# One program for three phases, with step 0 of attention begun in the last block of the first feed-forward phase

## The chip, the core and the metric

The kernel runs on one core of a Trainium2 chip. A core has five engines that run their own instruction queues in order and meet only at semaphores: TensorE (PE: multiplications and transposes; PEld is its weight load), VectorE (DVE), ScalarE (ACT), GpSimd (POOL), and SyncE (SP), which issues the transfers. The metric is the device time of one execution in microseconds (us).

## What is computed

A "macaron" layer over 4 sequences of 512 tokens, 256 wide, in float32: half a feed-forward step, attention, half a feed-forward step, each on the layer-normed x.

```python
x = x + 0.5 * ffn(layernorm(x))
x = x + attn(layernorm(x))
x = x + 0.5 * ffn(layernorm(x))
# ffn: 8 experts, silu(x @ W_e + b_e), the two best by the router's logits, weighted by a softmax,
#      then @ proj_w + proj_b, residual y = x + out, and RMS norm of y times norm_w
# attn: 16 heads of 128 in 4 groups that share a key and a value head, rotary embedding of q and k,
#       keys scaled by a weight per head, causal softmax, values, then @ wo.T
```

## The kernel before

Every multiplication is done in three parts: both operands are split into a rounded lead and a rest (names end in `hi`/`h` and `lo`/`l`), and lead x lead, lead x rest and rest x lead are summed in PSUM. ScalarE writes a lead (a copy that rounds), and VectorE or GpSimd subtracts it from the source to get the rest.

**Feed-forward** (`ffn_phase`, called twice: names f1_ and f2_). A body runs for each of the 4 blocks (sequences). A block has two halves g, and four pairs p of experts; a unit is one pair for 128 tokens. TensorE fills a ring of four PSUM banks with units, ScalarE takes the silu in place, VectorE adds the weighted halves into `acc` (`weighted`, L464), and TensorE may refill a bank when its unit is summed. Half a block later `acc` is transposed (`sum_T`, L794), split, and projected (`project`, L807 to L809); VectorE adds the residual, ScalarE squares, GpSimd raises to -0.5 (`inverse_rms`), VectorE scales (`scale_rows`) and GpSimd adds the rows into x (`add_rows`). Beside it run the layer norm of later blocks (`norm_stats`, `rstd`, `norm_rows`, `transpose_z`, `z_lead`, `z_rest`), the router, and, in the first phase, the split of attention's weights: the `group_lead` pieces on ScalarE and `group_rest` pieces on GpSimd, four pieces for each of four groups. Three groups go to a buffer in DRAM, `attn_split`, and group 0, the last, stays in `wa` and `gb` but for its output weights, which are stored from `gc` and loaded again by attention. The last block also normalises the two blocks 0 and 1 of attention, the second (j = BATCH + 1) by VectorE's z rows at L384 in the second half of the block.

The first phase ends with `step_project(0)` to `(5)`: key, four queries and value of step 0, each six matmuls of 128x512 into a bank of its own, which `step_out` on ScalarE copies to `ga` (raw) or `vT`. SyncE copies the halves of every raw part to `gc`, swapped, for the rotary embedding.

**Attention** (`attention_phase`, names at_). 16 steps, one for each group and sequence, of 4 heads. For each step the five raw parts (key and four queries) are rotated on GpSimd (raw x cos, swapped x sin, sum: L1063, L1065, L1069), their leads are written by ScalarE (L1291), their rests by GpSimd (L1054). A head is `scores`, `mask_min` on VectorE (L1152), `exps` on ScalarE (L1306), `normalise` on VectorE (L1161), `transpose_p`, leads and rests of the transposed probabilities, `weigh`, and `output`. Heads overlap: scores of head n + 2 stand beside the weighting of head n. Steps 1 to 14 run in hardware loops. Step 0 has its own start: rotations 0 and 2 and the rests 0, 1 and 2 on VectorE (`early_cos`, `early_sum`, `early_rest`: L1232 to L1243), rotations 1, 3 and 4 and the other rests on GpSimd.

**The order** is written out by hand, engine by engine. The three phases are three blocks of the language, with buffers and PSUM banks of their own beside a shared set; between two blocks all five engines meet at a barrier. Each block's first instructions set its constants and load ScalarE's table.

## Time and profile before

| | us |
|---|---|
| median of 3 runs | 856.11 |
| the runs | 856.01 to 856.42 |
| the profiled execution | 854.68 |
| its span | 852.8 |
| TensorE busy in the span | 802.1 (94%) |
| VectorE busy | 673.2 (79%) |
| ScalarE busy | 504.6 (59%) |
| GpSimd busy | 509.4 (60%) |

The span is what the profiler sees from first to last instruction; the time of the execution has 1.9 us around it. The first phase lasts to about 157 us, attention to about 721 us, the second feed-forward phase to the end. The page gives sums; the timeline gives each instruction's start and length and, in brackets, how long its engine was idle before it and what ended that. "PEq" or "DVEq" as releaser is the sequencer of the engine, here the barrier.

### The profile page before, as it was taken

How to read it: one execution, taken by the hardware profiler on the slowest of the kernel's cores; microseconds unless marked ns; L12 is line 12 of the kernel's file. 1: busy time of each engine (PE TensorE's matmuls, PEld its weight loads, DVE VectorE, ACT ScalarE, POOL GpSimd, SP SyncE). 2: the span in 40 equal slices, each digit the busy share in tenths (PEclk: the TensorE clock that was granted, in tenths of full speed). 3: DMA queues.
4: the chain of work that ended last, by engine and by line, in shares of the span. 5: the costliest groups of instructions: out<-in, count | busy, mean ns of one | idle time of the engine just before them, and what ended most of it. 6: DMA issues, size and time to landing. Idle time of an engine off the chain costs nothing. (4 is left out here: it accounts for less than half of the span.)

```text
span 852.8 us, 16061 instructions
## 1 busy us (share of the span) xinstructions
PE 802.1 (94%) x4712; PEld 702.2 (82%) x4712; DVE 673.2 (79%) x1929; ACT 504.6 (59%) x1241; POOL 509.4 (60%) x401
## 2 busy tenths in 40 slices
PE   7899997667999999999999999999999998899995
PEld 4688876556999999899999999999999997688884
DVE  5998996799786876966977868769678797988874
ACT  3455553355576765765766767658658674445442
POOL 4536632557777787777787877877877740312211
PEclk9899998879999999999999999999999999999997
DMA  9145411500212311312312213122221100000001
GB/s 300 51 149 185 139 48 58 141 13 13 51 38 61 99 25 37 98 30 68 98 25 49 74 37 86 37 74 49 74 49 44 30 13 1 1 1 25 25 1 50
DMA packets 29558, 52.19 MB, mean 61 GB/s; under 512 B 3922, under 2 KB 9682, under 8 KB 29522
## 3 DMA queue, kind: packets, MB, share of 16 engines
...
## 5 line engine op out<-in xcount | busy, mean ns | idle before, releaser
L1166 DVE TENSOR_TENSOR at_ptl<-at_pt,at_pth 128x512 fp32r<-128x512 f32 (+1 forms) x192 | 108.9, 594 | 47.1 <-ACT at_pth L1312 47.0
L1312 ACT ACTIVATE at_pth<-at_pt 128x512 fp32r<-128x512 f32 (+1 forms) x192 | 94.2, 525 | 84.8 <-PE at_pt L1470 84.8
L1306 ACT ACTIVATE at_pr<-at_pr,at_low 128x512 f32<-128x512 f32 (+3 forms) x256 | 140.6, 557 | 2.3 <-DVE at_low L1152 2.2
L1054 POOL TENSOR_TENSOR at_ql<-at_rot,at_qh 128x512 fp32r<-128x512 f32 x62 | 79.8, 1288 | 96.7 <-ACT at_qh L1291 96.7
L610 ACT ACTIVATE f_ex<-f_ex 128x512 f32<-128x512 f32 x128 | 74.5, 583 | 90.9 <-PE f_ex L782 90.3
L464 DVE SCALAR_TENSOR_TENSOR f_acc<-f_ex,f_full,f_acc 128x256 f32<-128x256 f32 x224 | 95.8, 477 | 26.2 <-ACT f_ex L610 25.4
L1161 DVE TENSOR_SCALAR at_pr<-at_pr,at_inv 128x128 f32<-128x128 f32 (+3 forms) x256 | 110.9, 494 | 2.3
L1069 POOL TENSOR_TENSOR at_rot<-at_rot,gc 128x512 f32<-128x512 f32 x78 | 101.5, 1302 | 8.1 <-POOLq L1086 2.1
L1063 POOL TENSOR_TENSOR at_rot<-ga,cos 128x512 f32<-128x512 f32 x78 | 102.0, 1308 | 4.1 <-POOL at_ql L1054 2.4
L1065 POOL TENSOR_TENSOR gc<-gc,sin 128x512 f32<-128x512 f32 x78 | 102.4, 1313 | 0.0
L1470 PE MATMUL at_pt<-ident,at_pr 128*128 128x128 f32 x640 | 94.2, 278 | 7.6 <-DVE at_pr L1161 6.7
L1152 DVE CUSTOM_DVE_ANT_0 at_pr<-at_sc,at_mask 128x512 f32<-128x512 f32 (+2 forms) x192 | 100.5, 547 | 0.0
L780 PE MATMUL f_ex<-f_e_hi,zh 128*128 128x512 f32 x224 | 93.5, 418 | 6.5 <-DVE f_acc L464 6.4
L1291 ACT ACTIVATE at_qh<-at_rot 128x512 fp32r<-128x512 f32 x64 | 40.5, 633 | 91.8 <-POOL at_rot L1069 89.7
L781 PE MATMUL f_ex<-f_e_hi,zl 128*128 128x512 f32 x224 | 90.9, 406 | 0.0
L782 PE MATMUL f_ex<-f_e_lo,zh 128*128 128x512 f32 x224 | 90.9, 406 | 0.0
L1484 PE MATMUL at_o<-at_pth,at_vh 128*128 128x512 f32 (+3 forms) x256 | 83.0, 324 | 0.1
L1486 PE MATMUL at_o<-at_pth,at_vl 128*128 128x512 f32 (+3 forms) x256 | 82.6, 323 | 0.0
L1485 PE MATMUL at_o<-at_ptl,at_vh 128*128 128x512 f32 (+3 forms) x256 | 82.4, 322 | 0.0
L1470 PEld LDWEIGHTS at_pt<-ident,at_pr 128*128 128x128 f32 x640 | 71.3, 143 | 10.4 <-DVE at_pr L1161 7.6
L1459 PE MATMUL at_sc<-at_keys,at_ql 128*128 (+4 forms) x256 | 78.7, 318 | 0.0
L1457 PE MATMUL at_sc<-at_keys,at_qh 128*128 (+3 forms) x192 | 71.9, 375 | 5.4 <-DVE at_ql L1243 5.4
...
## 6 DMA issues: line engine op xcount, KB each, us to landing
gc<-ga SPq DMA_DIRECT2D x160, 128.0 KB, 2.3
at_wo<-attn_split SPq DMA_DIRECT2D x8, 512.0 KB, 4.3
...
gb<-attn_split SPq DMA_DIRECT2D x6, 512.0 KB, 4.2
...
x<-in_x SPq DMA_DIRECT2D x4, 512.0 KB, 8.7
...
```

What stands on the lines that cost most here:

```text
L464: dve.scalar_tensor_tensor(out=acc[:, tile, :], in0=h, scalar=full_w[:, tile, e:e + 1], in1=acc[:, tile, :], op0=ALU.mult, op1=ALU.add).th ...
L780: pe.matmul(o, zh[:, c, tok], hi[:, :, w], start=(c == 0), stop=False)
L781: pe.matmul(o, zl[:, c, tok], hi[:, :, w], start=False, stop=False)
L1063: pool.tensor_tensor(rot[r % 2][:], raw[r], cosT[:], ALU.mult)
L1065: pool.tensor_tensor(swap[r], swap[r], sinT[:], ALU.mult).then_inc(sin_done, 1)
L1069: pool.tensor_tensor(rot[r % 2][:], rot[r % 2][:], swap[r], ALU.add).then_inc(sum_done, 1)
L1152: dve.tensor_tensor_reduce(out=out, in0=sc[bank][:, col:col + w], in1=masked, scale=1.0, scalar=3e38, op0=ALU.add, op1=ALU.min, accum_out= ...
L1161: dve.tensor_scalar(a, a, inv[h % 2][:, i:i + 1], None, ALU.mult).then_inc(nm_done, 1)
L1166: dve.tensor_tensor(ptl[h % 2][:, cols], pt[(NF * h + k) % 2][:, 0:FLEN[k]], pth[h % 2][:, cols].bitcast(F32), ALU.subtract).then_inc(lo_d ...
L1306: act.activation(pr[h % 2][:, cols], pr[h % 2][:, cols], ACT.Exp, bias=low[h % 2][:, i:i + 1], scale=-1.0, accum_out=tot[h % 2][:, i:i + 1 ...
L1312: act.activation(pth[h % 2][:, cols], pt[(NF * h + k) % 2][:, 0:FLEN[k]], ACT.Copy).then_inc(hi_done, 1)
L1470: r = pe.transpose(pt[(NF * h + k) % 2][:, col + (i - kt) * P:col + (i - kt + 1) * P], pr[h % 2][:, OFF[i] + kt * P:OFF[i] + (kt + 1) * P] ...
```

## The change

1. There is one block. The phases are now functions (`feed_forward`, `attention`) that return a program for each engine, and each engine runs the three in a row. Where two interleave, a program is a generator that stops at `yield`. Both barriers go, and with them the constants' second and third setting.
2. The eight PSUM banks have one set of names (`pj`, `sc`, `pt`, `o`) and each phase maps its own onto them. All but the last projection of step 0 go through the bank `pj1`; each waits until ScalarE has copied the one before. Buffers in SBUF are laid out anew (`ROOMS` leaves space), so that step 0 can write while the first phase still reads.
3. Projections 0, 1 and 2 of step 0 stand inside the last block's second half. ScalarE's leads of the rotated key and first query stand there too, among the silus, and VectorE's rests of them. The last projections, scores of heads 0 and 1, and the tail of the last block are interleaved.
4. GpSimd does all five rotations of step 0, VectorE the rests 0, 1 and 2, GpSimd the rests 3 and 4.
5. The split of group 0 begins with the output weights, written straight to `wo`: two stores and two loads of 512 KB go. Slots of the last group move: 25, 26, 27, 28.
6. The statistics and rows of the last extra normalisation come earlier in VectorE's queue.
7. At the end of attention, the second phase's table load, the lead and rest of expert pair 1 and its first router multiplication are put into the last attention step.

```diff
+ROOMS = (256, 2800, 384)
...
 
-        SLOTS = ((3, 4, 5, 6), (9, 10, 12, 13), (17, 18, 20, 21), (25, 26, 28, 29))
+        SLOTS = ((3, 4, 5, 6), (9, 10, 12, 13), (17, 18, 20, 21), (25, 26, 27, 28))
 
         def piece_at(i, g, p):
...
@@ -320,10 +319,13 @@
                     scale_queries(i)
                 if first:
                     group_rest(i, 0)
+                if first and i == LAST:
+                    rstd(BATCH + 1)
+                if first:
                     group_rest(i, 1)
                 if i > 0:
                     inverse_rms(i - 1, 1)
-                if i + 2 < NORMS:
+                if i + 2 < NORMS and i < LAST:
                     rstd(i + 2)
                 if i > 0:
                     add_rows(i - 1, 1)
...
@@ -512,10 +516,14 @@
                     add_residual(i - 1, 1)
                 if i + 1 < NORMS:
                     z_rest(i + 1)
+                if first and i == LAST:
+                    norm_stats(BATCH + 1)
                 weighted(i, 0, 3)
                 if i > 0:
                     mean_square(i - 1, 1)
-                if i + 2 < NORMS:
+                if first and i == LAST:
+                    norm_rows(BATCH + 1)
+                elif i + 2 < NORMS:
                     norm_stats(i + 2)
                 if first and i == 0:
                     dve.wait_ge(p_hi_done, 1)
@@ -524,8 +532,6 @@
                 if i > 0:
                     scale_rows(i - 1, 1)
                 sum_rest(i, 0)
-                if i == LAST and NORMS > BATCH:
-                    norm_rows(BATCH + 1)
                 weighted(i, 1, 1)
                 if i < LAST:
                     choose(i + 1)
@@ -535,11 +541,13 @@
                 if i < LAST:
                     weigh_chosen(i + 1)
                 add_residual(i, 0)
+                if first and i == LAST:
+                    early_rest(dve, 0)
                 weighted(i, 1, 3)
                 mean_square(i, 0)
-
-            if not first:
-                dve.sem_inc(e_lo_done, 1)
+                if first and i == LAST:
+                    early_rest(dve, 1)
+
             if first:
                 dve.memset(r_hl[:].bitcast(F32), 0.0).then_inc(setup, 1)
                 dve.memset(r_h0[:].bitcast(F32), 0.0).then_inc(setup, 1)
...
@@ -643,11 +665,10 @@
 
                 act.wait_ge(step_done, k + 1)
                 if k < NR:
-                    if k == 0:
-                        act.wait_ge(a_lo_done, PIECES * KV)
-                    act.activation(raw[k], step_ps[k][:], ACT.Copy).then_inc(raw_done, 1)
+                    act.wait_ge(a_lo_done, PIECES * KV - (1 if k < 2 else 0))
+                    act.activation(raw[k], t_ps[1][:], ACT.Copy).then_inc(raw_done, 1)
                 else:
-                    act.activation(vT[:], step_ps[k][:], ACT.Copy).then_inc(vt_done, 1)
+                    act.activation(vT[:], pj[0][:], ACT.Copy).then_inc(vt_done, 1)
 
             def body(i):
                 silu(i, 0, 0, 0)
@@ -681,23 +702,33 @@
                 group_lead(i, 1, 0)
                 silu(i, 1, 0, 1)
                 sum_lead(i, 0)
+                if first and i == LAST:
+                    step_out(0)
                 silu(i, 1, 1, 0)
                 group_lead(i, 1, 1)
                 silu(i, 1, 1, 1)
-                if i == LAST and NORMS > BATCH:
+                if first and i == LAST:
                     z_lead(BATCH + 1)
+                    step_out(1)
                 silu(i, 1, 2, 0)
+                if first and i == LAST:
+                    rotated_lead(act, 0, 0)
                 if i < LAST:
                     half_tanh(i + 1)
                 group_lead(i, 1, 2)
                 silu(i, 1, 2, 1)
+                if first and i == LAST:
+                    step_out(2)
                 silu(i, 1, 3, 0)
                 squares(i, 0)
+                if first and i == LAST:
+                    rotated_lead(act, 0, 1)
                 silu(i, 1, 3, 1)
 
             if not first:
                 act.sem_inc(e_hi_done, 1)
-            act.wait_ge(half_set, 2)
+            if first:
...
@@ -812,19 +843,27 @@
             def step_project(k):
 
                 if k == 0:
-                    pe.wait_ge(zlo_done, C * NORMS)
-                    pe.wait_ge(a_lo_done, PIECES * KV)
-                elif k < NR:
-                    pe.wait_ge(acc_done, sums_of(UNITS * BATCH - RING + k - 1))
+                    pe.wait_ge(zlo_done, C * (BATCH + 1))
+                    pe.wait_ge(a_lo_done, PIECES * KV - 2)
+                elif k == NR:
+                    pe.wait_ge(raw_done, NR + 1)
                 else:
-                    pe.wait_ge(raw_done, 1)
+                    pe.wait_ge(raw_done, k)
+                    pe.wait_ge(a_lo_done, PIECES * KV - (2 if k < 2 else 0))
                 (hi, lo), w = ((wa[:, 0], wa[:, 1]), k) if k < 2 else (wb, k - 2)
                 w = slice(w * HD, (w + 1) * HD)
+                bank = (pj[0] if k == NR else t_ps[1])[:]
                 for c in range(C):
-                    pe.matmul(step_ps[k][:], hi[:, c, w], zh[:, c, 0:SEQ], start=(c == 0), stop=False)
-                    pe.matmul(step_ps[k][:], hi[:, c, w], zl[:, c, 0:SEQ], start=False, stop=False)
-                    r = pe.matmul(step_ps[k][:], lo[:, c, w], zh[:, c, 0:SEQ], start=False, stop=(c == C - 1))
+                    pe.matmul(bank, hi[:, c, w], zh[:, c, 0:SEQ], start=(c == 0), stop=False)
+                    pe.matmul(bank, hi[:, c, w], zl[:, c, 0:SEQ], start=False, stop=False)
+                    r = pe.matmul(bank, lo[:, c, w], zh[:, c, 0:SEQ], start=False, stop=(c == C - 1))
                 r.then_inc(step_done, 1)
+
+            def ring_free():
+                pe.wait_ge(acc_done, sums_of(UNITS * BATCH - RING))
+
+            def rows_scaled(g):
+                pe.wait_ge(xn_done, BT * LAST + HT * (g + 1))
 
             def body(i):
                 if i > 0:
@@ -843,11 +882,16 @@
                 sum_T(i, 0)
                 if i < LAST:
                     logits_back(i + 1)
+                elif first:
+                    step_project(0)
                 experts(i, 1, 1)
-                if i == LAST and NORMS > BATCH:
+                if first and i == LAST:
                     transpose_z(BATCH + 1)
+                    step_project(1)
                 experts(i, 1, 2)
                 project(i, 0)
+                if first and i == LAST:
+                    step_project(2)
                 experts(i, 1, 3)
 
             if first:
...
@@ -1097,14 +1131,19 @@
             rest(STEPS - 1, NR - 1)
             rstd(2)
 
-        @block.vector
-        def _(dve):
+        def offsets(dve):
             dve.sem_inc(wa_in, WA0)
             dve.sem_inc(wb_in, WB0)
+            dve.sem_inc(wo_in, WO0)
             dve.sem_inc(lo_done, LO0)
             dve.sem_inc(ol_done, OL0)
 
+        def vector(dve, tail, last_pairs):
+            sum_rest, scale_rows, add_residual, mean_square, add_last_rows, rows_final = tail
+
             def norm_stats(k, b, _):
+                if k < 2:
+                    rows_final(b)
                 if k == 2:
                     dve.wait_ge(xu_done, 2 * (STEPS - BATCH + b + 1))
                 for t in range(BT):
...
+            last_block = BATCH - 1
+            sum_rest(last_block, 1)
             dve.wait_ge(mask_in, 16)
             mask_min(0, 0)
+            early_rest(dve, 2)
+            scale_rows(last_block, 0)
             norm_stats(*NORMS[0])
+            add_residual(last_block, 1)
             normalise(0, 0)
+            mean_square(last_block, 1)
             mask_min(1, 1)
+            scale_rows(last_block, 1)
+            add_last_rows()
+            value_rest(0)
             prob_rest(0, 0, 0)
             prob_rest(0, 0, 1)
+            normalise(1, 1)
+            prob_rest(0, 0, 2)
             norm_stats(*NORMS[1])
-            normalise(1, 1)
-            value_rest(0)
-            prob_rest(0, 0, 2)
             step(0, True, False)
             with dve.Fori(1, STEPS - 1) as s:
                 step(s, False, False)
             step(STEPS - 1, False, True)
             add_output(STEPS - 1, part=1)
 
-        @block.scalar
-        def _(act):
...
-            act.activation(warm[:], mhalf[:], ACT.Exp).then_inc(half_set, 1)
-            rotated_lead(0, 0)
-            rotated_lead(0, 1)
+                        last_pairs()
+
+            act.activation(warm[:, 2], mhalf[:], ACT.Exp)
+            step_out(3)
+            sum_lead(BATCH - 1, 1)
+            rotated_lead(act, 0, 2)
+            step_out(4)
+            exps(0, 0)
+            squares(BATCH - 1, 1)
             raw_out(1, 0)
+            rotated_lead(act, 0, 3)
+            step_out(NR)
             raw_out(1, 1)
-            rotated_lead(0, 2)
-            rotated_lead(0, 3)
-            exps(0, 0)
+            exps(1, 1)
             value_lead(0)
-            raw_out(1, 2)
             prob_lead(0, 0, 0)
             prob_lead(0, 0, 1)
-            rotated_lead(0, 4)
-            exps(1, 1)
+            raw_out(1, 2)
+            rotated_lead(act, 0, 4)
             prob_lead(0, 0, 2)
             step(0, True, 2)
             with act.Fori(1, STEPS - 2) as s:
@@ -1381,8 +1414,9 @@
             step(STEPS - 2, False, 1)
```

The second half of block 3 on ScalarE, from the lead of its first sums (`f1_ch`), before; `f1_ex` and later `pj`, `sc` are the ring's banks, `f1_t` and `pt`, `o` the others:

```order
L614 ACTIVATE f1_ch<-f1_t0 128x512 [waits f1_ct_done]
L610 ACTIVATE f1_ex2<-f1_ex2 128x512 [waits f1_ex_done]
L640 ACTIVATE gc<-ga 128x1024 [waits f1_a_in3,f1_a_in2]
L610 ACTIVATE f1_ex3<-f1_ex3 128x512 [waits f1_ex_done]
L586 ACTIVATE zh<-f1_t0 128x512 [waits f1_tz_done]
L586 ACTIVATE zh<-f1_t1 128x512 [waits f1_tz_done]
L610 ACTIVATE f1_ex0<-f1_ex0 128x512 [waits f1_ex_done]
L610 ACTIVATE f1_ex1<-f1_ex1 128x512 [waits f1_ex_done]
L610 ACTIVATE f1_ex2<-f1_ex2 128x512 [waits f1_ex_done]
L620 ACTIVATE f1_sq,f1_ss<-f1_wide0 128x256 [waits f1_yadd_done]
L620 ACTIVATE f1_sq,f1_ss<-f1_wide0 128x256
L610 ACTIVATE f1_ex3<-f1_ex3 128x512 [waits f1_ex_done]
```

And after:

```order
L634 ACTIVATE f1_ch<-pt0 128x512 [waits f1_ct_done]
L669 ACTIVATE ga<-pj1 128x512 [waits f1_a_lo_done,f1_step_done]
L630 ACTIVATE sc1<-sc1 128x512 [waits f1_ex_done]
L630 ACTIVATE sc2<-sc2 128x512 [waits f1_ex_done]
L606 ACTIVATE zh<-pt0 128x512 [waits f1_tz_done]
L606 ACTIVATE zh<-o 128x512 [waits f1_tz_done]
L669 ACTIVATE ga<-pj1 128x512 [waits f1_a_lo_done,f1_step_done]
L630 ACTIVATE pj0<-pj0 128x512 [waits f1_ex_done]
L1298 ACTIVATE at_keys<-at_rot0 128x512 [waits at_sum_done]
L630 ACTIVATE sc0<-sc0 128x512 [waits f1_ex_done]
L669 ACTIVATE ga<-pj1 128x512 [waits f1_a_lo_done,f1_step_done]
L630 ACTIVATE sc1<-sc1 128x512 [waits f1_ex_done]
```

Two copies of raw projections to `ga` and the lead of the rotated key stand ahead of the last silus; before, all six copies came behind them.

GpSimd at the same place, before, from the power for the norm of block 5 (`f1_rs`):

```order
L267 TENSOR_TENSOR f1_rs<-f1_ve,f1_mhalf 128x4 [waits f1_ln_var]
L308 TENSOR_TENSOR x<-x,f1_y 128x512 [waits f1_xn_done]
L298 TENSOR_TENSOR gb<-ga,gb 128x512 [waits f1_a_hi_done]
L298 TENSOR_TENSOR gc<-ga,gc 128x1024 [waits f1_a_hi_done]
L303 TENSOR_TENSOR f1_rr<-f1_ms,f1_mhalf 128x2 [waits f1_rms]
L308 TENSOR_TENSOR x<-x,f1_y 128x512 [waits f1_xn_done]
L303 TENSOR_TENSOR f1_rr<-f1_ms,f1_mhalf 128x2 [waits f1_rms]
L77 UNCONDITIONAL_BRANCH
L1048 UNCONDITIONAL_BRANCH [waits barrier_Pool_Activation_PE_DVE_SP_gather]
L1081 MEMSET at_mhalf 128x4
L1063 TENSOR_TENSOR at_rot1<-ga,cos 128x512 [waits at_half_set,raw_done]
```

And after, from the rest of the piece `wa`:

```order
L297 TENSOR_TENSOR wa<-ga,wa 128x512 [waits f1_a_hi_done]
L302 TENSOR_TENSOR rr<-ms,mhalf 128x2 [waits f1_rms]
L307 TENSOR_TENSOR x<-x,f1_y 128x512 [waits f1_xn_done]
L297 TENSOR_TENSOR gb<-ga,gb 128x512 [waits f1_a_hi_done] x2
L1100 TENSOR_TENSOR at_rot0<-ga,cos 128x512 [waits raw_done]
L1102 TENSOR_TENSOR gc<-gc,sin 128x512 [waits swap_in0]
L1104 TENSOR_TENSOR at_rot0<-at_rot0,gc 128x512 [waits at_sin_done]
L1100 TENSOR_TENSOR at_rot1<-ga,cos 128x512 [waits raw_done]
L1102 TENSOR_TENSOR gc<-gc,sin 128x512 [waits swap_in1]
L1104 TENSOR_TENSOR at_rot1<-at_rot1,gc 128x512 [waits at_sin_done]
L302 TENSOR_TENSOR rr<-ms,mhalf 128x2 [waits f1_rms]
```

The rotations (L1100 to L1104) follow the last pieces directly, and the power for the last block's first half (`rr`) stands behind two of them.

TensorE in the last attention step, after: the end of the output multiplication of three heads, the router's four, and the weighting of head 3 (`at_pth1`); before, the router's rows stood behind the barrier:

```order
L1549 MATMUL pj1<-at_wo1,at_oh 128x256
L1550 MATMUL pj1<-at_wo0,at_ol 128x256
L783 MATMUL sc2<-zh,r_hl 128x512 [waits at_zlo_done]
L784 MATMUL sc2<-zl,r_h0 128x512
L783 MATMUL sc2<-zh,r_hl 128x512
L784 MATMUL sc2<-zl,r_h0 128x512
L1518 MATMUL o<-at_pth1,at_vh 128x512 [waits at_lo_done,at_ol_done]
L1519 MATMUL o<-at_ptl1,at_vh 128x512
```

The router waits for the rests of the normalised rows (`at_zlo_done`) in the middle of the attention step.

## Rows read from the trace of the kernel before

**Rows 1.** Page, parts 1 and 2: busy time; busy tenths in 40 slices of 21.3 us.
```profile
PE 802.1 (94%) x4712; PEld 702.2 (82%) x4712; DVE 673.2 (79%) x1929; ACT 504.6 (59%) x1241; POOL 509.4 (60%) x401
...
PE   7899997667999999999999999999999998899995
...
POOL 4536632557777787777787877877877740312211
```

**Rows 2.** Waits of PE, 120 to 240 us: us in total, times, longest.
```profile
PE f_t L735 <- DVE z L384: 5.7, 1, 5.7
PE at_pt L1470 <- DVE at_pr L1161: 5.6, 2, 4.1
PE at_sc L1457 <- DVE at_ql L1243: 5.4, 1, 5.4
PE at_pj L1396 <- DVE z L1124: 4.0, 1, 4.0
PE at_pj L1405 <- DVEq L1102: 1.9, 1, 1.9
```

**Rows 3.** Windows: us, busy us of each engine, PEclk, DMA share, GB/s.
```profile
173.00:190.00 17.00, 10.56 (x41) 8.59 (x40) 16.59 (x48) 8.97 (x25) 10.69 (x9) 0.71 0.07 15
...
400.00:420.00 20.00, 20.00 (x130) 18.32 (x129) 15.38 (x47) 13.50 (x36) 16.58 (x14) 1.00 0.19 49
```

**Rows 4.** Timeline of PE at the first seam: start us, us, engine, line, instruction, [idle before].
```profile
126.05 0.60 PE L794 MATMUL f_t<-ident,f_acc 128*128 128x128 f32 x4
...
144.98 0.39 PE L824 MATMUL f_t<-zh,wa 128*128 128x512 f32 x1
...
146.36 0.40 PE L824 MATMUL f_ex<-zh,wa 128*128 128x512 f32 x1
...
165.55 0.79 PE L1457 MATMUL at_sc<-at_keys,at_qh 128*128 128x512 f32 x1 [5.38 <-DVE at_ql L1243]
...
180.17 0.78 PE L1457 MATMUL at_sc<-at_keys,at_qh 128*128 128x512 f32 x1
```

**Rows 5.** Timeline of DVE, 130 to 190 us, the same columns.
```profile
128.83 0.87 DVE L492 SCALAR_TENSOR_TENSOR f_y<-f_wide,f_rr,rows 128x256 f32<-128x256 f32 x2
...
130.21 4.91 DVE L384 TENSOR_SCALAR z<-x,f_mv,f_rs 128x256 f32<-128x256 f32 x4
...
189.05 1.37 DVE L1124 TENSOR_SCALAR z<-x,at_mv,at_rs 128x256 f32<-128x256 f32 x4
```

**Rows 6.** Page, part 5: groups of ACT, all through the program.
```profile
L1306 ACT ACTIVATE at_pr<-at_pr,at_low 128x512 f32<-128x512 f32 (+3 forms) x256 | 140.6, 557 | 2.3 <-DVE at_low L1152 2.2
```

**Rows 7.** Timeline of POOL, 127 to 160 us.
```profile
127.42 1.01 POOL L267 TENSOR_TENSOR f_rs<-f_ve,f_mhalf 128x4 f32<-128x4 f32 x1 [1.22 <-DVE f_ve L372]
...
157.34 1.29 POOL L1063 TENSOR_TENSOR at_rot<-ga,cos 128x512 f32<-128x512 f32 x1 [0.18 <-POOL at_mhalf L1081]
158.58 1.74 POOL L1065 TENSOR_TENSOR gc<-gc,sin 128x512 f32<-128x512 f32 x1
```

**Rows 8.** Issues of DMAs, 120 to 200 us: count, KB each, median us to landing.
```profile
gc<-ga SPq DMA_DIRECT2D x16, 128.0 KB, 2.3
...
at_wo<-attn_split SPq DMA_DIRECT2D x2, 512.0 KB, 4.9
```

**Rows 9.** Timelines of PE, DVE and ACT at the second seam.
```profile
721.48 0.47 PE L756 MATMUL f_t<-zh,r_hl 128*128 128x512 f32 x1 [1.05 <-PEq L900]
...
732.64 0.47 PE L780 MATMUL f_ex<-f_e_hi,zh 128*128 128x512 f32 x1 [3.31 <-DVE f_acc L464]
...
728.22 2.35 DVE L425 TENSOR_SCALAR f_w<-f_th 128x4 f32<-128x4 f32 x1
...
717.06 0.60 ACT L1316 ACTIVATE at_oh<-at_o 128x512 fp32r<-128x512 f32 x1 [3.39 <-PE at_o L1486]
721.51 1.28 ACT L701 ACT_TABLE_LOAD   x1 [3.85 <-PEq L900]
...
722.91 1.04 ACT L605 ACTIVATE f_e_hi<-e_raw 128x1024 fp32r<-128x1024 f32 x1
```

406 lines of the change are left out of this document (225 added, 181 removed).

## The prediction

> **What bounds the kernel now.** I read the page first. TensorE is busy 94% of the span, and its strip in 40 slices is at 9 nearly everywhere; the holes lie at slices 7 to 10 (128 to 213 us) and again near slice 35 [rows 1]. So only work that stands in TensorE's way at those holes can shorten the span. The windows confirm the contrast: at 400 to 420 us TensorE is busy all 20.00 us at a granted clock of 1.00, at 173 to 190 us it is busy 10.56 of 17 us at 0.71 [rows 3]. Then the list of TensorE's waits from 120 to 240 us says what the holes are: 5.7 us for the normalised rows of the block that step 0 will read, 1.9 us for the barrier between the first feed-forward phase and attention, 5.4 us for the first rests of rotated keys and queries, 5.6 us for normalised probabilities, 4.0 us for the z rows of a later block, together 22.6 us [rows 2]. Last, the timelines show why. From 135 to 157 us GpSimd is almost empty (its strip falls to 5 and 3 tenths there) [rows 1], yet the rotations of step 0, which are GpSimd's kind of work, begin at 157.34, behind the barrier [rows 7]; TensorE reaches the first scores of step 0 at 165.55 and the third scores (head 2) at 180.17 [rows 4]. The second seam is small: 1.05 us before TensorE's router multiplication and 3.31 us later for the first weighted sums [rows 9].
>
> I call the time of the start of the third scores the milestone. Behind it step 0 runs as before, so what the milestone gains, the span gains.
>
> **The change at the first seam, in order of time on the clock of the trace before.** Work is moved, hardly any is removed: six projections of 1.38 us each (144.98 to 146.36) [rows 4], two barriers, two stores of 512 KB and their two loads back. TensorE pays the same multiplications, so the gain is waiting alone, and I follow the chain.
>
> Start: sum transposes at 126.05 [rows 4]. VectorE now does the statistics of the extra normalisation (about 2.0 us) before the weighted sums that this transpose waits for, and GpSimd holds the piece of wa behind the power for that normalisation (1.01 us) [rows 7]. I estimate 0.6 and 0.4 us of new TensorE waiting; the first projection ends near 128.9.
>
> The normalised rows themselves took 4.91 us at 130.21, when GpSimd was running three multiplications and subtractions beside them, and 1.37 us at 189.05 when it was not [rows 5]. In the new order they stand earlier, when GpSimd has one short piece to do; I take 1.8 us, so the 5.7 us wait goes. What is late next is the last pieces of the weight split: GpSimd adds the scaled rows first. These were scaled by 129.7 (128.83 and 0.87) [rows 5]; with 1.3 us more of VectorE work ahead, 131.0. Add 1.3 us for the addition and 1.3 us for the piece: 133.6. ScalarE's copy of projection 0 waits for that piece, since it overwrites its source, and all of ScalarE's queue, two silus first, waits behind it. The copy is out at 134.2. TensorE, with one bank for all projections, waits 1.5 us for it. Then TensorE is busy to 145.3.
>
> Rotation 0: the half swap lands some 3.1 us after the copy (issue 0.6, 2.3 to landing [rows 8], 0.2 between); then sine product and addition, 1.3 us each as the cosine product took 1.29 [rows 7]: 139.9. ScalarE waits for it ahead of the silu of unit 13, so the weighted sums slip. By the order of ScalarE's queue (lead 0, silu, copy 2, silu, squares, lead 1, silu) its last silu ends at 145.2, the last weighted sum at 146.5, the rest of query 0 at 147.3. The first scores start there, against 165.55.
>
> Then the gain shrinks, since VectorE now does only the rests and GpSimd all five rotations. Rotation 2 is queued behind the power for the last rows: start 147.35, three operations of 1.3, end 151.3. ScalarE waits for it ahead of the exponentials of head 0: four at 0.557 mean [rows 6], 2.3 us, 154.8. The squares of the last rows wait on VectorE's addition (statistics of another block stand before it) to 156.3; squares, power, and only then rotation 3: 158.4 to 162.3. ScalarE waits for rotation 3 ahead of the value copy and the exponentials of head 1; these end at 166.4, value lead and rest, the first probability rest at 168.4. The milestone is at **168.6** against 180.17: a gain of 11.6 us. Two of the operations in the chain may run at the 1.74 us of 158.58 rather than 1.29 [rows 7], 0.9 us: I take 11.
>
> Cover: with three loads fewer on the queue the swaps meet less traffic; the mask load, moved ahead, has some 10 us until it is used. If all TensorE waits of the seam went, the gain would be 17.1 us of idle (5.7, 1.9, 5.4 and the longest of 4.1 before probabilities [rows 2]) and, I estimate from the granted clock of 0.71 in 17 us [rows 3], about 4 us of slow matmuls: 21 us. If only the barrier went, it would be 1.9 us. I take 11, nearest to the row-by-row chain.
>
> After the milestone the wait of 4.0 us for z rows stays: it is VectorE beside GpSimd's rotations, and those stand there as before.
>
> **The change at the second seam.** The router's four matmuls go ahead of the last weighting, so the barrier wait of 1.05 us goes [rows 9] and nothing on TensorE is added. VectorE then can choose experts right after the logits, with the second pair's split behind it already, an operation of the length of ScalarE's 1.04 us for the same elements [rows 9]: weights 1.0 us earlier, the wait of 3.31 us falls to about 2.3. The 2.35 us for a 4-element product at 728.22 [rows 9] stays, since GpSimd's residual starts at the same event. ScalarE's table load (1.28 us) and the split of 1.04 us now stand ahead of the last lead of attention; ScalarE was idle 3.39 us there [rows 9], they take 2.5, so nothing is late. Gain 2.0 us, bounds 1 and 4.4.
>
> On that cover the trace shows the load at 1.28 us with the next instruction right behind it. The Trainium skill, page "ScalarE: Activation LUTs", section "What ACT_TABLE_LOAD costs", adds a drain and gives 2.66 us for a switch; by it ScalarE would be 0.5 us late there and the second seam would give 1.5 us. The measured row decides for me.
>
> **Sum.** 11 and 2 us: 13 us. The profiled execution took 854.68 us, span 852.8 and 1.9 around it; its new span would be 839.8. The median of the runs is 856.11, 1.4 above the profiled one; from the median I predict 843.1 us.
>
> **Rivals.**
> First, the forecast: gain of 9 to 17 us, 839 to 847 us, chance 0.60.
> Second, more: ScalarE's waits ahead of silus and exponentials hurt less than I laid out, because rotations end before ScalarE comes to them, and the z wait of 4.0 us [rows 2] moves to where GpSimd is idle. 13, 4 and 2 us of slower clock: 19 us, 837 us; chance 0.13. For it: those waits are in my arithmetic, not in the trace. Against: GpSimd's three queued operations per rotation are firm.
> Third, less: the swap of rotation 0 takes 4.9 us as the large loads do [rows 8], 2.6 more, and GpSimd's chained operations run at 1.74, twelve times 0.45, of which half is on the path: 5.3 us back, 848.4 us; chance 0.15, as far as 853.
> Fourth, slower: VectorE and GpSimd block each other. Four z rows took 4.91 instead of 1.37 us beside GpSimd, 0.9 us each [rows 5]. From 126 to 168 us the new order puts some 20 VectorE operations of these kinds (z rows, rests, normalised probabilities, the row addition) near 15 operations of GpSimd which used to run before or behind. If 15 of the 20 are hit and all on the path, 13.5 us go and the gain is spent; with all 20 it is 18 us and 861 us. Chance 0.07. For it: the sizes are measured. Against: most of these stand where the chain waits for GpSimd anyway.
> The Trainium skill, page "SBUF — State Buffer", section "SBUF: two separate sides", says this as a rule that speaks against the change: VectorE's fast modes, and its operations with two SBUF inputs against a GpSimd reader, take one port pair by turns for whole instructions. The 4.91 us agree with it; it gives no price of its own.
> Fifth, within 0.2%: chain and seams cancel, 0.05.
>
> **How the numbers follow.** About 0.2%, 1.7 us, is what a measurement of this kernel can tell from no change. Faster 0.88, same 0.05, slower 0.07. The range leaves out the slower cases and the ends of the second and third: 835.5 to 851.
>
> **What would show it.** Right: no barrier gap at 155 us; first scores near 147 us, third scores between 167 and 172; router matmuls inside the last attention step; the wait for weighted sums in the second phase 2 to 3 us; the middle of attention unchanged pass for pass. Wrong: third scores after 176 us, or ScalarE idle under 1 us ahead of the leads of rotations 0, 2 and 3, or any change of the attention loop's pass time.

## The result and the profile after

The changed kernel took **842.86 us** (median of 4 runs, 841.95 to 843.60) against 856.06 us (4 runs, 854.50 to 856.42): a ratio of **0.985, 95% interval 0.983 to 0.987**. Forecast were 843.1 us and the range 835.5 to 851. The profiled execution took 843.1 us, its span is 841.1 (before 854.68 and 852.8), so the traces differ by 11.7 us.

Page of the changed kernel, parts 1 and 2, the lines of [rows 1]:

```profile
PE 796.0 (95%) x4712; PEld 699.4 (83%) x4712; DVE 659.6 (78%) x1923; ACT 503.2 (60%) x1241; POOL 513.7 (61%) x403
...
PE   7899998777999999999999999999999999899995
...
POOL 4545736775778778777777787877777750312211
```

TensorE has the same 4,712 multiplications. Its hole in the eighth to tenth slice reads 777 where it read 667, and the seventh slice reads 8 where it read 7. Waits of TensorE from 120 to 240 us in the changed kernel, the answer to [rows 2] (us in total, times, longest; the rows from 1.2 us up):

```profile
PE pj L1430 <- DVE z L1163: 6.8, 2, 3.9
PE pj L857 <- ACT ga L1321: 2.5, 1, 2.5
PE pt L1504 <- DVE at_ptl L1205: 1.9, 2, 1.5
PE pj L1474 <- ACT vT L671: 1.9, 1, 1.9
PE pt L1504 <- DVE at_pr L1200: 1.6, 1, 1.6
PE pj L857 <- ACT ga L669: 1.6, 1, 1.6
PE pt L823 <- DVE f_acc L468: 1.3, 2, 1.0
PE pj L1439 <- DVE zl L1174: 1.2, 2, 1.0
```

The barrier, the 5.7 us for the normalised rows of the first phase and the 5.4 us for the first rests are gone. Other waits stand in their place: ScalarE's copies of the projections (`ga`, `vT`), and z rows of later blocks, 6.8 us where there were 4.0. TensorE's timeline in the changed kernel (start us, length, ..., [idle before <- releaser]), for [rows 4]:

```profile
126.20 0.66 PE L823 MATMUL pt<-ident,f_acc 128*128 128x128 f32 x4 [0.28 <-DVE f_acc L468]
...
146.82 0.50 PE L1491 MATMUL sc<-at_keys,at_qh 128*128 128x512 f32 x1
...
168.21 0.48 PE L1491 MATMUL sc<-at_keys,at_qh 128*128 128x512 f32 x1
...
208.97 0.60 PE L1474 MATMUL pj<-ident,vT 128*128 128x128 f32 x4
...
681.04 0.60 PE L1474 MATMUL pj<-ident,vT 128*128 128x128 f32 x4
...
722.31 0.76 PE L809 MATMUL sc<-f_e_hi,zh 128*128 128x512 f32 x1 [3.38 <-DVE f_acc L468]
...
829.20 0.66 PE L823 MATMUL pj<-ident,f_acc 128*128 128x128 f32 x4 [1.98 <-DVE f_acc L468]
```

The first row is the sum transposes from which the prediction counted, the second the first scores (forecast 147.3), the third the milestone (forecast 168.6). The transposes of `vT` begin steps 1 and 15 of attention, the last two rows end the wait at the second seam and the second phase. With the same events of the kernel before, of which this document has not yet shown the last,

```profile
220.84 0.60 PE L1440 MATMUL at_pj<-ident,vT 128*128 128x128 f32 x4
...
689.98 0.60 PE L1440 MATMUL at_pj<-ident,vT 128*128 128x128 f32 x4
...
840.88 0.66 PE L794 MATMUL f_t<-ident,f_acc 128*128 128x128 f32 x4 [1.97 <-DVE f_acc L464]
```

the span divides as follows. (z transposes: the first of the second phase, 711.80 and 702.89 us.)

| stretch | before | after | difference |
|---|---|---|---|
| start to sum transposes | 126.05 | 126.20 | +0.15 |
| to third scores (first seam) | 54.12 | 42.01 | **-12.11** |
| to step 1 | 40.67 | 40.76 | +0.09 |
| steps 1 to 14 | 469.14 | 472.07 | **+2.93** |
| step 15, to the z transposes | 21.82 | 21.85 | +0.03 |
| second seam, to the end of the ring wait | 20.84 | 19.42 | **-1.42** |
| second phase, to its last sum transposes | 108.24 | 106.89 | **-1.35** |
| the end | 11.92 | 11.90 | -0.02 |

The first seam did what was forecast. But the loop, which "stays pass for pass", gives back 2.9 us, and the second phase, of which nothing was said, gains 1.35. The first row hides a gain too: in this trace the clock fell at a bad place, which costs 1.2 us (last section).

### The profile page after: what moved, and what is told of

The parts are those of the page before. It is cut to its first block, busy times and chain, and to the rows that moved or that the text cites. A ratio compares the mean times of both kernels' runs of the same rounds, so it can differ in the third digit from the quotient of the medians.

```text
span 841.1 us, 16039 instructions
## 1 busy us (share of the span) xinstructions
PE 796.0 (95%) x4712; PEld 699.4 (83%) x4712; DVE 659.6 (78%) x1923; ACT 503.2 (60%) x1241; POOL 513.7 (61%) x403
## 4 chain that ended last, share of the span: by engine, by line
PE 78%; DVE 12%; issue 3%; POOL 3%; ACT 2%; DMA 1%; SPq 0%; POOLq 0%; DVEq 0%; ACTq 0%
PE pt L1504 8%; PE pj L1439 5%; PE pj L1441 5%; PE pj L1440 5%; PE o L1518 5%; PE o L1520 5%; PE o L1519 5%; PE sc L1493 4%; PE pj L1548 4%; PE sc L1491 4%; PE sc L1492 4%; PE pj L1549 4%; PE pj L1550 4%; PE sc L809 3%; PE sc L811 3%
## 5 line engine op out<-in xcount | busy, mean ns | idle before, releaser
L1342 ACT ACTIVATE at_pth<-pt 128x512 fp32r<-128x512 f32 (+1 forms) x192 | 93.8, 524 | 81.7 <-PE pt L1504 81.7
L1205 DVE TENSOR_TENSOR at_ptl<-pt,at_pth 128x512 fp32r<-128x512 f32 (+1 forms) x192 | 109.1, 596 | 42.5 <-ACT at_pth L1342 42.4
L1104 POOL TENSOR_TENSOR at_rot<-at_rot,gc 128x512 f32<-128x512 f32 x80 | 103.3, 1292 | 6.3
L1100 POOL TENSOR_TENSOR at_rot<-ga,cos 128x512 f32<-128x512 f32 x80 | 104.0, 1300 | 2.4 <-POOL at_ql L1092 2.4
L1191 DVE CUSTOM_DVE_ANT_0 at_pr<-sc,at_mask 128x512 f32<-128x512 f32 (+2 forms) x192 | 100.8, 550 | 0.0
L1504 PE MATMUL pt<-ident,at_pr 128*128 128x128 f32 x640 | 92.5, 275 | 4.6 <-DVE at_pr L1200 2.7
L1518 PE MATMUL o<-at_pth,at_vh 128*128 128x512 f32 (+3 forms) x256 | 82.9, 324 | 0.1
L1519 PE MATMUL o<-at_ptl,at_vh 128*128 128x512 f32 (+3 forms) x256 | 82.4, 322 | 0.0
L1520 PE MATMUL o<-at_pth,at_vl 128*128 128x512 f32 (+3 forms) x256 | 82.3, 321 | 0.0
L1493 PE MATMUL sc<-at_keys,at_ql 128*128 (+4 forms) x256 | 76.8, 311 | 0.0
L1504 PEld LDWEIGHTS pt<-ident,at_pr 128*128 128x128 f32 x640 | 70.5, 140 | 7.1 <-DVE at_pr L1200 3.2
L1548 PE MATMUL pj<-at_wo,at_oh 128*128 128x256 f32 x248 | 71.7, 289 | 0.0
L1549 PE MATMUL pj<-at_wo,at_oh 128*128 128x256 f32 x248 | 70.2, 283 | 0.0
```

What stands on the lines that cost most here:

```text
L1100: pool.tensor_tensor(rot[r % 2][:], raw[r], cosT[:], ALU.mult)
L1205: dve.tensor_tensor(ptl[h % 2][:, cols], pt[(NF * h + k) % 2][:, 0:FLEN[k]], pth[h % 2][:, cols].bitcast(F32), ALU.subtract).then_inc(lo_d ...
L1493: r = pe.matmul(o, ql(h)[:, q], k_hi, start=False, stop=True)
L1504: r = pe.transpose(pt[(NF * h + k) % 2][:, col + (i - kt) * P:col + (i - kt + 1) * P], pr[h % 2][:, OFF[i] + kt * P:OFF[i] + (kt + 1) * P] ...
L1518: pe.matmul(o, vh[:, kt, :], pth[h % 2][:, a], start=(kt == 0), stop=False)
L1519: pe.matmul(o, vh[:, kt, :], ptl[h % 2][:, a], start=False, stop=False)
```

## The experiments

Each kernel is named by what it does; its ratio is to the kernel before on the same chip. "Seam time" is the time from the sum transposes near 125 us to the third scores, as in the table.

**1. Without the early start.** The changed kernel, but step 0 is begun behind the last unit of the block: projections 0 to 2, their copies, two leads and two rests move there, one edit on each engine.

```diff
-                elif first:
-                    step_project(0)
...
-                if first and i == LAST:
-                    step_project(2)
...
+                step_project(0)
+                step_project(1)
+                step_project(2)
```

> The changed kernel with nothing of step 0 inside the last block: projections 0 to 2, their copies, the leads of key and query 0 and their rests stand behind the last expert unit; no barrier, everything else as changed. My theory (the gain is one chain of projection, copy, swap, rotation, lead, rest, and it starts with the first copy): the first copy comes at about 139 us instead of 133.3, the first scores near 151 instead of 146.8, the third scores 3 to 4 us later than 168.2, and the kernel takes 846 to 847.5 us. Rival 'barriers': the gain comes from the two barriers, their reloads and the DRAM trips alone, and the early start is worth nothing: 843 us. Rival 'early start is all of it': back at 850 us or more.

848.54 us (848.01 to 848.98), ratio 0.9915 [0.9895, 0.9935]: 5.7 us slower than the changed kernel. The seam time is 49.46 us, so 7.5 of the 12.1 us belong to the early start, more than expected: rotation, lead and rest are now in full view of TensorE. The medians show less of it, and so do the two profiled executions (5.8): in this trace the sum transposes start at 124.81 us, 1.4 earlier, which is the clock of the last section. Its first scores:

```profile
152.29 0.79 PE L1483 MATMUL sc<-at_keys,at_qh 128*128 128x512 f32 x1 [5.60 <-DVE at_ql L1295]
```

That is the 5.38 us of [rows 4] again. Taking away the barrier alone does not take away the wait that stood behind it; putting feed-forward work beside the chain does.

**2. No interleaving at the second seam.** The second phase's table load, lead, rest and router multiplication wait until attention is through; the barrier stays away.

```diff
-            step_programs[2](dve, next(one[2](dve)), lambda: next(second))
+            step_programs[2](dve, next(one[2](dve)), lambda: None)
...
-            step_programs[3](act, next(one[3](act)), lambda: next(second))
+            step_programs[3](act, next(one[3](act)), lambda: None)
...
-            step_programs[4](pe, next(one[4](pe)), lambda: next(second))
+            step_programs[4](pe, next(one[4](pe)), lambda: None)
```

> The changed kernel with the second phase begun behind attention: router, table load and split of expert pair 1 come after the last attention instruction of each engine, without a barrier. My theory (second seam worth about 1.5 to 2 us, most of it by earlier weights): 1.2 to 2 us slower than the changed kernel, 844.2 to 845 us, with the wait for the weighted sums back at 3.3 us or more. Rival: only the barrier counted, and the order at this seam is worth nothing: 843 us.

842.69 us (842.58 to 842.89), ratio 0.9849 [0.9830, 0.9869]; from the z transposes to the end of the ring wait 19.43 us, against 19.42 in the changed kernel and 20.84 before. The theory fell as far as the end of the ring wait: all of the gain there stays without the interleaving. That wait ends with VectorE's weights, and these are held up further on (see "Second seam" below).

Behind the ring wait this trace is slower, 108.14 us to the last sum transposes against 106.89 (and 106.82 to 106.94 in the other traces whose expert weights lie at the same place), though its end is 0.6 us shorter. TensorE's next wait, in the changed kernel and then in this one:

```profile
727.40 0.66 PE L762 MATMUL pj<-ident,z 128*128 128x128 f32 x4 [0.65 <-DVE z L388]
```

```profile
726.28 1.06 PE L762 MATMUL pj<-ident,z 128*128 128x128 f32 x4 [2.12 <-DVE z L388]
```

VectorE has these rows ready equally long after the ring wait in both. In the changed kernel the multiplications before them stand 0.43 us apart and fill the wait; here they stand 0.23 us apart, TensorE waits, and the 0.43 us come behind, on work that is waited for. That is once more the clock of the last section. Whether the missing interleaving moved it there is not shown: it is one trace, and the medians of the two kernels are 0.2 us apart.

**3. Norm rows back in their old place.** Statistics, power and rows of the last extra normalisation stand late again; the rows' part of the edit:

```diff
-                if first and i == LAST:
-                    norm_rows(BATCH + 1)
-                elif i + 2 < NORMS:
+                if i + 2 < NORMS:
...
                 sum_rest(i, 0)
+                if first and i == LAST:
+                    norm_rows(BATCH + 1)
```

> The changed kernel with statistics, power and rows of the extra normalisation where they were before (rows behind the first sums' rest in the second half of block 3). My theory (VectorE and GpSimd take turns there): the four z rows take over 3.5 us again instead of 1.38, TensorE's transposes of them start near 135 instead of 131.3, and the kernel is 1 to 3 us slower, 844 to 846 us. Rival: ScalarE's wait for the last weight pieces bounds this stretch anyway and hides the rows: within 0.5 us of the changed kernel.

846.63 us (845.78 to 846.84), ratio 0.9895 [0.9876, 0.9915]: 3.8 us slower than the changed kernel. The seam time is 47.0 us, 5.0 longer. VectorE's z rows, first in the changed kernel, then in this one:

```profile
126.85 1.38 DVE L388 TENSOR_SCALAR z<-x,mv,rs 128x256 f32<-128x256 f32 x4
```

```profile
129.70 4.80 DVE L386 TENSOR_SCALAR z<-x,mv,rs 128x256 f32<-128x256 f32 x4
```

The same four rows take 4.80 instead of 1.38 us, and TensorE waits 4.4 us for them again. Moving one normalisation by some 3 us gives 5.0 us at the seam and 3.8 of the 13 in the medians. With the 7.5 us of number 1 that is as much as the whole 12.1; no run puts the first barrier back alone, so its own share is not shown.

**4. Rests 0 to 2 on GpSimd.** `early_rest` on VectorE is taken out, and GpSimd does the rest right behind each rotation.

```diff
-                if first and i == LAST:
-                    early_rest(dve, 0)
...
-            early_rest(dve, 2)
...
+            rest(0, 0)
...
+            rest(0, 1)
...
+            rest(0, 2)
```

> The changed kernel with rests 0, 1 and 2 of step 0 on GpSimd, each behind its rotation, instead of on VectorE. My theory (GpSimd's queue is the chain from 134 to 168 us): each rest adds its 1.3 us and the wait for ScalarE's lead, about 2 us each, of which the idle stretches of GpSimd at 143 and 151 us take up some; third scores 3 to 5 us later, 846 to 848 us. Rival (VectorE with two operands from SBUF against GpSimd costs as much): within 1 us of 843.

842.73 us (842.37 to 843.64), ratio 0.9847 [0.9828, 0.9867]: no difference in the medians, and the theory of 3 to 5 us fell. The seam time is 42.72 us, 0.7 longer, less than the spread of the runs. The three rests cost GpSimd 1.3 us each, but GpSimd had been waiting. Two rows of the changed kernel's GpSimd, then the two at the same place of this one:

```profile
146.25 1.08 POOL L302 TENSOR_TENSOR rr<-ms,mhalf 128x2 f32<-128x2 f32 x1 [2.83 <-DVE ms L486]
147.31 1.29 POOL L1100 TENSOR_TENSOR at_rot<-ga,cos 128x512 f32<-128x512 f32 x1
```

```profile
147.95 0.71 POOL L302 TENSOR_TENSOR rr<-ms,mhalf 128x2 f32<-128x2 f32 x1 [0.60 <-DVE ms L486]
148.63 1.29 POOL L1096 TENSOR_TENSOR at_rot<-ga,cos 128x512 f32<-128x512 f32 x1
```

Idle time of 2.83 us ahead of the power has become 0.60. So the rests on VectorE (item 4 of the change) are worth 0.7 us at the seam and nothing that the medians show.

**5 to 7. Two better orders, and both.** Behind the last power stands rotation 3, though it needs nothing from it; and the last two pieces of the weight split stand behind a row addition that nobody waits for. Number 5 puts the power behind the rotation, number 6 the addition behind the pieces, number 7 does both.

```diff
-            inverse_rms(BATCH - 1, 1)
...
+            inverse_rms(BATCH - 1, 1)
```

```diff
-                if i > 0:
+                if i > 0 and not (first and i == LAST):
                     add_rows(i - 1, 1)
...
+                if first and i == LAST:
+                    add_rows(i - 1, 1)
```

> The changed kernel with rotation 3 of step 0 ahead of the power for the last rows in GpSimd's queue (it stood behind it and began at 158.17). My theory (ScalarE's 5.08 us of idle at 162.39 and TensorE's 1.92 and 1.54 us behind it come from that place in GpSimd's queue): rotation 3 starts near 154.8 and ends near 158.9, third scores 3 us earlier, near 165, 839.5 to 841 us. Rival: the last rows' power, now 1.4 us later, or the z rows behind it give it back: 842 to 844 us.

> The changed kernel with the last two pieces of the weight split ahead of the addition of the block's scaled rows in GpSimd's queue in block 3. My theory (ScalarE's 5.76 us before the first copy at 133.25, with all silus behind it, comes from that place): copy 0 near 129, TensorE's wait of 1.56 us gone, first scores 2 us earlier, near 144.7, third scores near 166, 840 to 841.5 us. Rival: the swap and GpSimd's three operations bound rotation 2 and 3 anyway: within 0.7 us of 842.9.

> The changed kernel with both moves in GpSimd's queue: pieces ahead of the row addition, rotation 3 ahead of the power. My theory (one chain, two separate delays): the gains add, third scores 5 us earlier, near 163, 837.5 to 839 us. Rival: once one is gone the other is hidden: no better than the better of the two alone, 840 us.

Number 5: 840.72 us (840.34 to 841.39), 0.9818 [0.9793, 0.9843]. Number 6: 841.23 (841.09 to 841.41), 0.9822 [0.9798, 0.9846]. Number 7: 840.78 (839.95 to 841.54), 0.9819 [0.9793, 0.9844]. Singly they are 2.1 and 1.6 us below the changed kernel's median, and 2.0 and 1.5 below number 8 (next), which has the old order and ran on the same chip; together they seem to add nothing. GpSimd of number 5, where the cosine product of rotation 3 begins at 153.47 instead of 158.17 us (3.4 us earlier, counted from the sum transposes):

```profile
152.22 1.29 POOL L307 TENSOR_TENSOR x<-x,f_y 128x512 f32<-128x512 f32 x1 [2.25 <-DVE f_y L496]
153.47 1.26 POOL L1100 TENSOR_TENSOR at_rot<-ga,cos 128x512 f32<-128x512 f32 x1
...
158.19 0.71 POOL L302 TENSOR_TENSOR rr<-ms,mhalf 128x2 f32<-128x2 f32 x1 [0.77 <-DVE ms L486]
```

But the seam times are 41.36, 41.19 and 40.55 us against 42.01: gains of 0.65, 0.82 and 1.46. At the seam they do add. My rival for number 7 was right in the time and wrong in the reason: the third scores did come earlier. In the traces number 7 is 0.32 us shorter than number 5; the other 0.5 us of the seam's 0.8 went into a loop of 472.36 instead of 472.02 us and an end 0.2 us longer. The four runs of each spread over 1.1 and 1.6 us and cannot tell such differences, and why the medians of 5 and 6 fell by more than the seam did is not shown.

**8. Attention's buffers 256 bytes lower.** Why is the loop slower? Pass times are 33.6 or 33.84 us before (mixed) and 33.9 after, and the whole difference stands in the output multiplications (`pj <- at_wo, oh`, 256 columns): mean spacing over the 48 of a pass 115.5 or 120.0 ns before, 122.1 after, at a granted clock of 1.00 in both. A first test moved all that is laid out behind the gap in attention.

```diff
-ROOMS = (256, 2800, 384)
+ROOMS = (192, 2800, 384)
```

> The changed kernel with the space in attention's buffer layout 192 elements instead of 256, so that queries 2 and 3, probabilities, values and head outputs lie 256 bytes lower in each partition and nothing else moves. Theory 'addresses' for the attention pass that takes 33.91 us instead of 33.6 to 33.84: the output matmuls change from 122 ns and the pass by 0.1 to 0.3 us, 1.4 to 4 us in all. Theory 'neighbours' (which instructions of other engines run beside the output matmuls): 122 ns and 33.91 us stay, 842.9 us.

842.68 us (841.88 to 843.44), 0.9842 [0.9817, 0.9867], spacing 121.5 to 122.1 ns: nothing changed. Each of these multiplications has two operands in SBUF: a block of 128x128 of the heads' outputs (`oh`, `ol`), which TensorE loads first, and the output weights `wo`, whose 256 columns then stream through. `oh` had moved; `wo` lies ahead of the gap and had not.

**9 to 11. The weights moved, in both kernels, and one more instruction.** I worked out where each operand lies. In bytes from a multiple of 512, `wo` is at 192 before and 384 after, the expert weights (which stream as well, in 512 columns) at 320 and 384. Number 9 gives the changed kernel `wo` at 192; number 10 gives the kernel before `wo` and expert weights at 384; number 11 leaves every address and adds an instruction to TensorE's queue in each step.

```diff
+        sb("pad0", [P, 80])
         wo = [sb(f"wo{n}", [P, G, D], F32R) for n in range(2)]
-        sb("gap", [P, room])
+        sb("gap", [P, room - 80])
```

```diff
+        sb("pad0", [P, 48])
         wo = [sb(f"wo{n}", [P, G, D], F32R) for n in range(2)]
...
+        sb("pad1", [P, 80])
         pth = [sb(f"pth{n}", [P, TRI], F32R) for n in range(2)]
...
+        sb("pad0", [P, 16])
         e_hi, e_lo = sb("e_hi", [P, E, C * D], F32R), sb("e_lo", [P, E, C * D], F32R)
```

```diff
             def value_T(t, after_key):
+                pe.wait_ge(vt_done, t + 1).then_inc(passed, 1)
```

> The changed kernel with one edit of layout: attention's output weights stand 320 bytes further on, so that their offset from a multiple of 512 bytes is 192 as in the kernel before (it is 384 in the changed kernel); all else of attention and of the feed-forward phases stays where it was. The address theory: the 122 ns spacing of the output multiplications (115.5 or 120 in the kernel before) comes from where these weights lie, so it falls to 115 to 120 ns, a pass of the loop from 33.9 to 33.6 to 33.85 us, and the time to 840 to 841.5 us. The rival, that it is something in the stream of instructions: 122 ns, 33.9 us, 842 to 843.5 us.

> The kernel before with its layout moved: attention's output weights 192 bytes on (offset 384 from a multiple of 512, as in the changed kernel; attention's output operand keeps its offset 384), and the expert weights of both feed-forward phases 64 bytes on (offset 384 as in the changed kernel, 320 in the kernel before). The address theory: output multiplications 122 ns apart instead of 115.5 or 120, expert multiplications 228 instead of 233 ns, so a slower loop (3 us) and faster feed-forward phases (1.6 us), 857.5 us. The rival: 115.5 and 120 ns, 233 ns, 856.3 us, nothing changed.

> The changed kernel with one more instruction in TensorE's queue in every step of attention, ahead of the value's transposes: a wait for the same event as the instruction behind it waits for, so it holds nothing up. If the stream of instructions sets the spacing (where the loop's instructions lie, or when they are fetched), the output multiplications change from a constant 122 ns to another value, or to two values as in the kernel before, 115 to 121 ns, and the time goes to 839 to 842. If addresses set it: 122 ns, a pass at most 0.05 us longer, 842.5 to 844 us.

The operand's rows for `wo` in the kernel before, the changed one, number 9 and number 10 (count, then shortest, median and longest duration in ns):

```profile
L1514 PE MATMUL at_pj<-at_wo,at_oh x248: 276/276/393, 226.9 to 718.6; 128*128 128x256 f32 x124
```

```profile
L1548 PE MATMUL pj<-at_wo,at_oh x248: 277/283/388, 215.0 to 711.0; 128*128 128x256 f32 x124
```

```profile
L1549 PE MATMUL pj<-at_wo,at_oh x248: 276/280/388, 214.5 to 708.6; 128*128 128x256 f32 x124
```

```profile
L1517 PE MATMUL at_pj<-at_wo,at_oh x248: 278/283/388, 226.5 to 721.3; 128*128 128x256 f32 x124
```

And the expert weights' rows, kernel before and number 10:

```profile
L780 PE MATMUL f_ex<-f_e_hi,zh x224: 391/397/795, 16.5 to 838.0; 128*128 128x512 f32 x112
```

```profile
L781 PE MATMUL f_ex<-f_e_hi,zh x224: 387/389/795, 16.5 to 839.6; 128*128 128x512 f32 x112
```

| | before | number 10 | after | number 9 | number 11 |
|---|---|---|---|---|---|
| spacing of output multiplications, ns | 115.5, 120 | 121.7 to 122.1 | 121.9 to 122.1 | 120, 115.5 | 121.7 to 122.1 |
| steps 1 to 14, us | 469.14 | 472.05 | 472.07 | 470.43 | 472.02 |
| spacing of expert multiplications, 40 to 125 us, ns | 233.3 | 227.8 | 227.8 | 227.8 | 227.8 |
| second phase, us | 108.24 | 106.94 | 106.89 | 106.87 | 106.89 |

The edit of the kernel before that moves nothing but addresses turns its loop into the changed kernel's loop to 0.02 us, and its second phase to 0.05 us. The two effects go in opposite ways, so its time hardly moves: 856.42 us (10 runs) against 855.45 (13 runs), 1.0015 [0.9997, 1.0033]. Its pads shift more than the two weights, though: keys, queries, values and probabilities go from 192 to 384 with `wo`, and the feed-forward buffers behind the expert weights by 64 bytes. Number 9 moves `wo` alone. Number 9 wins back 1.6 us of the loop, 840.76 us (840.15 to 842.03), 0.9830 [0.9802, 0.9859]; of twelve whole passes it has one at 115.5 ns and the rest at 120, where the kernel before has eight at 115.5. Number 11 took 842.24 us (842.03 to 842.68), 0.9848 [0.9820, 0.9875], with the spacing as it was. So addresses decide, not the stream of instructions. For 1.6 of the 2.9 us it is the address of `wo` alone; for the other 1.3 no run says which operand, and of what the expert multiplications read, only the weights moved. Which property of an address counts, and why passes at one address differ, stays open: two places of each of the weights were tried, no more.

**12. Three edits together.** Both orders of number 7, and `wo` moved as in number 9.

> The changed kernel with three edits together: rotation 3 ahead of the last power, pieces 2 and 3 of the weight split ahead of the row addition, and attention's output weights 320 bytes further on. The three act at different places (the third scores come 0.65 and 0.8 us earlier against the sum transposes by the first two, the loop is 1.6 us shorter by the third), so my theory says they add: from 842.8 us by 3.1 us to 839.7 us, 839 to 840.5, with a pass of the loop of 33.6 to 33.85 us. The rival, that gains at the seam are covered by another wait again: 840.8 us and more, as the first two together gave.

839.28 us (836.72 to 840.70), 0.9823 [0.9803, 0.9843]: the lowest median of all, and near the 839.7 us of the sum. But the kernel before was faster too on this chip (855.03), and the ratio is no better than those of numbers 5 to 7; its interval and the changed kernel's (0.9832 to 0.9866) still touch. What adds up is seen in the trace: the loop takes 470.34 us, as with `wo` moved alone. Its profiled execution was the shortest run, 836.7 us, with a seam time of 38.91 us against number 7's 40.55, though both have the same order there. Windows of 155 to 160 us (us; busy us and instructions of PE, PEld, DVE, ACT, POOL; granted clock; DMA share; GB/s), number 7 and then number 12:

```profile
155.00:160.00 5.00, 4.08 (x12) 3.21 (x13) 4.97 (x17) 2.10 (x6) 4.15 (x5) 0.69 0.23 54
```

```profile
155.00:160.00 5.00, 4.10 (x25) 3.57 (x25) 4.97 (x17) 3.08 (x7) 4.15 (x5) 1.00 0.24 56
```

Up to 156.7 us the two agree within 0.05 us. Then number 7's multiplications of 512 columns stand 0.43 us apart, those of number 12 0.23: 12 against 25 in the window. The copy of the value projection is 0.5 us later, and the copy behind it, with the exponentials of head 1, 1.6 us. In number 12 TensorE falls to the lower level some 7 us later. Number 9 keeps the full level in this window too and falls behind it, and its seam time is 42.83 us, 0.8 longer than the changed kernel's. These are the two kernels of this order with `wo` moved; whether that or the run chose the place, two traces do not say.

## Why the prediction was right, and where it was not

- **A reading.** From 135 to 157 us GpSimd's strip in [rows 1] stands at 2 and 5 tenths, not at 5 and 3. The argument holds: GpSimd is busy 2.7 of those 22 us.
- **Start and z rows.** Right. The rows took 1.38 us (1.8 assumed), and experiment 3 puts 5.0 us of the seam on their place.
- **Copy of projection 0, rotation 0, first scores.** The copy was out at 133.9 (134.2 forecast) after TensorE had waited 1.6 us (1.5), rotation 0 at 139.6 (139.9), the first scores began at 146.8 (147.3). The order on ScalarE was read rightly too; its row ahead of rotation 2's lead is `[3.81 <-POOL at_rot L1104]`.
- **Rotation 3 behind the power.** It ended at 162.4 (162.3), and was worth 0.65 us at the seam when put ahead, with a median 2.1 us lower (experiment 5). That order was on the list of the chain; it was not named as something to mend.
- **Milestone.** Seam time 12.1 us shorter. The sum of the rows said 11.6; I took 11 for operations at 1.74 us, which did not come. A rounding down by caution, not a step that failed.
- **"After the milestone the wait of 4.0 us for z rows stays."** Mis-sized: two waits, 6.8 us in all. Of the two sets of rows in this stretch the first took 1.37 us before [rows 5] and the second 3.96, beside GpSimd; now both stand beside GpSimd:

```profile
175.26 3.81 DVE L1163 TENSOR_SCALAR z<-x,at_mv,at_rs 128x256 f32<-128x256 f32 x4
...
187.59 3.78 DVE L1163 TENSOR_SCALAR z<-x,at_mv,at_rs 128x256 f32<-128x256 f32 x4
```

  The second wait was foreseen (2.9 us, 4.0 before), the first is new. It cost nothing on balance: waits for probabilities went from 5.6 to 1.6 us, and the table's stretch to step 1 is unchanged (+0.09 us).
- **Second seam, 2.0 us.** Measured 1.42. The barrier's 1.05 us went; the weights did not come 1.0 us earlier, and the ring wait is 3.38 us, as long as before, not 2.3. The step that failed is "VectorE then can choose experts right after the logits, with the second pair's split behind already": the split was not what held VectorE up. Before, it ended as the logits arrived, whose transposes end at 725.15 us; now VectorE waits 1.14 us for them. From the first operation on the logits to the end of the ring wait both traces take 7.46 us, so the gain lies ahead of the logits. VectorE and TensorE before, then VectorE after:

```profile
723.99 1.23 DVE L444 TENSOR_TENSOR f_e_lo<-e_raw,f_e_hi 128x1024 fp32r<-128x1024 f32 x1 [2.83 <-ACT f_e_hi L605]
725.18 0.19 DVE L403 TENSOR_TENSOR f_l<-f_t,r_off 128x32 f32<-128x32 f32 x1
...
724.49 0.66 PE L763 MATMUL f_t<-ident,f_rT 128*128 128x128 f32 x4 [0.50 <-ACT f_rT L590]
```

```profile
714.85 0.19 DVE L407 TENSOR_TENSOR l<-sc,r_off 128x32 f32<-128x32 f32 x1 [1.14 <-PE sc L790]
```

  Behind the logits stand, as before, the split of the next pair, 1.22 us, and the slow product:

```profile
716.54 1.22 DVE L448 TENSOR_TENSOR f_e_lo<-e_raw,f_e_hi 128x1024 fp32r<-128x1024 f32 x1
...
717.88 2.36 DVE L429 TENSOR_SCALAR w<-th 128x4 f32<-128x4 f32 x1
```

```profile
717.84 2.37 POOL L273 TENSOR_TENSOR f_zres<-z,rows 128x1024 f32<-128x1024 f32 x1 [22.72 <-DVE f_e_lo L448]
```

  A product of 4 elements lasts as long as GpSimd's residual of 1,024 that started 0.04 us ahead of it. I had written that this stays; it does.
- **The table load.** The Trainium skill, page "ScalarE: Activation LUTs", section "What ACT_TABLE_LOAD costs", adds a drain to the load. After this load the next instruction follows at once, so the measured row was rightly preferred:

```profile
704.77 1.28 ACT L732 ACT_TABLE_LOAD   x1
706.07 0.20 ACT L732 ACTIVATE warm<-warm 128x4 f32<-128x4 f32 x1
```

- **"The middle of attention unchanged pass for pass."** Wrong by 2.93 us, 0.21 a pass. I had named a change of pass time as a sign against the prediction and given it no price. It is addresses (experiment 10), 1.6 us of it that of `wo` (experiment 9): a part of the change that its list names (item 2, buffers laid out anew) and that I had costed at nothing without saying so.
- **The feed-forward phases** were not in the sum: -1.35 us in the second, the address of the expert weights. The first gains by it as well: its expert multiplications stand 227.8 ns apart for 233.3 (from the sums near 41 us to those near 125 number 10 takes 84.19 us, the kernel before 85.64), and where the clock falls early the sum transposes start at 124.96 us (number 8), 1.1 earlier than before.
- **The books.** Forecast 11 and 2. Found at the seams 12.1 and 1.4, in the feed-forward phases 1.1 and 1.35, given back in the loop 2.9: 13.0 us, and 13.2 in the medians. The profiled execution of the changed kernel holds 1.2 us of a clock that fell at a bad place (last section), so the traces differ by 11.7 only. So a good part of the closeness to 843.1 is luck: unforeseen terms of opposite sign, -2.4 and +2.9, and an under-estimate of 1.1 at the first seam against an over-estimate of 0.6 at the second.
- **The rivals.** "More" failed since ScalarE's waits were real (3.81 and 5.1 us ahead of the leads of rotations 2 and 3). "Less" needed swaps of 4.9 us or slower rotations: neither came. "Slower" had its mechanism right, since z rows do take 3.8 and 4.8 us beside GpSimd, and its reach wrong: the changed order takes the set of 4.91 us out of the way and slows another from 1.37 to 3.81, in the place of a wait that was there already. The Trainium skill, page "SBUF — State Buffer", section "SBUF: two separate sides", gives the rule for this: VectorE's fast modes and GpSimd take one port pair by turns, for whole instructions. The traces agree in so far as rows that take 1.37 us alone take 3.8 to 4.9 beside GpSimd; which mode the rows run in, no run here shows.
